# One fused conv-attention and mixture-of-experts kernel: order of ScalarE's token work, an earlier start of the token statistics, and a matrix product that adds the two output halves

## The reference, cut to what matters

```python
x = x + conv_attention(layernorm_c(x))        # 8 heads, 8x8 windows, plus a 3x3 local conv; q, k, v, out are 1x1
t = tokens(x)                                 # 8192 tokens of 64 numbers
gate_logits = layernorm(t) @ Wg + bg          # 8 experts
top_w, top_i = top_k(gate_logits, 2); top_w = softmax(top_w)
t = t + sum over the two experts e of top_w[e] * (gelu(layernorm(t) @ W1[e] + b1[e]) @ W2[e] + b2[e])
```

## Time and profile before

| | |
|---|---|
| median of 3 runs | 451.93 us (451.66 to 452.38) |
| the profiled execution, its own time | 450.36 us |
| its span, first to last instruction | 448.6 us |
| mean granted TensorE clock | 0.974 |
| busy PE, DVE, ACT, POOL | 409.8, 351.9, 334.9, 304.3 us |

### The profile page before, as it was taken

How to read it: one execution, slowest core, us unless ns; L and a number is a source line. 1 busy time by engine, 2 the same in 40 slices (tenths; PEclk the granted TensorE clock), 3 DMA queues, 4 the chain that set the end, 5 groups by cost and what they waited for, 6 DMA issues and landing times. The chain is left out here.

```text
span 448.6 us, 12510 instructions
## 1 busy us (share of the span) xinstructions
PE 409.8 (91%) x3921; PEld 277.0 (62%) x3921; DVE 351.9 (78%) x1240; ACT 334.9 (75%) x889; POOL 304.3 (68%) x406
## 2 busy tenths in 40 slices
PE   6897989899999899899899789698999999999995
PEld 5354434445454444445445345245999999999995
DVE  4688979977888978868969989888876688778532
ACT  2466688788877787777787665444988898888884
POOL 4233434775855889888888858466777777777765
PEclk8899989999999999989999899989999999999998
DMA  9916800000000000000000000014332222222310
GB/s 221 233 48 124 183 2 2 1 1 1 2 1 2 14 20 20 21 18 14 20 21 14 24 26 32 19 49 105 99 75 76 64 58 59 62 71 73 78 45 0
DMA packets 36168, 22.42 MB, mean 50 GB/s; under 512 B 13648, under 2 KB 33855, under 8 KB 36104
## 3 DMA queue, kind: packets, MB, share of 16 engines
q1 hardware_dynamic: 30264, 14.70, 14.7%
q0 software_dynamic: 4960, 6.45, 4.4%
q10 hardware_dynamic: 880, 0.48, 0.7%
HBM read 13.07 MB, written 9.27 MB: 50 GB/s over the span
## 5 line engine op out<-in xcount | busy, mean ns | idle before, releaser
L672 POOL TENSOR_TENSOR pn<-pe_,rs 128x512 f32<-128x512 f32 x64 | 67.2, 1050 | 65.4 <-DVE rs L1213 61.3
L1509 PE MATMUL bank<-aa,bd 64*64 64x256 f32 x512 | 70.5, 392 | 12.2 <-ACT pt L821 8.7
L642 POOL DMA_INDIRECT rows_hbm<-rowb,posu x64 | 65.7, 1026 | 23.2 <-issue 17.2
L687 POOL DMA_INDIRECT out<-bt,zs x63 | 62.8, 996 | 21.5 <-issue 16.1
L1512 PE MATMUL bank<-pt,bt 64*64 64x256 f32 x512 | 70.5, 393 | 0.0
L1202 DVE TENSOR_REDUCE mx<-bank 128x8 f32<-128x512 f32 x64 | 43.8, 684 | 31.4 <-PE bank L1509 31.0
L833 ACT ACTIVATE pe_<-sc 128x512 f32<-128x512 f32 x64 | 40.6, 635 | 33.2 <-DVE sc L1205 23.0
L1509 PEld LDWEIGHTS bank<-aa,bd 64*64 64x64 f32 x512 | 33.5, 133 | 46.0 <-issue 35.7
L793 ACT COPY zs<-bank 128x512 f32<-128x512 f32 x64 | 37.2, 581 | 15.0 <-PE bank L1512 14.9
L1205 DVE TENSOR_TENSOR sc<-bank,mx 128x512 f32<-128x512 f32 x64 | 44.2, 691 | 2.2
L1325 DVE SCALAR_TENSOR_TENSOR bt<-bank,zs 128x64 f32<-128x64 f32 x91 | 25.4, 280 | 25.6 <-PE bank L1692 24.3
(11 more groups left out here) (298 smaller groups left out, 1042.0 us busy)
## 6 DMA issues: line engine op xcount, KB each, us to landing
zs<-rows_hbm SPq DMA_DIRECT2D x91, 66.0 KB, 2.2
wloc<-in_L_conv_w_local SPq DMA_DIRECT2D x2, 1152.0 KB, 8.8
rows_hbm<-zrow SPq DMA_DIRECT2D x1, 1914.0 KB, 13.6
x_sb<-in_x SPq DMA_DIRECT2D x3, 512.0 KB, 10.9
wloc<-in_L_ffn_W SPq DMA_DIRECT2D x2, 512.0 KB, 6.8
rows_hbm<-rowb,posu POOLq DMA_INDIRECT x64
out<-bt,zs POOLq DMA_INDIRECT x63, 2.3
wrec<-in_w2b SPq DMA_DIRECT2D x1, 520.0 KB, 4.3
```

Of the source, the lines that this page charges most:

```text
L642: nc.gpsimd.indirect_dma_start(out=rows_hbm, out_offset=bass.IndirectOffsetOnAxis(ap=posu[:, t:t + 1], axis=0), in_=rowb[:, t], in_offset= ...
L672: nc.gpsimd.tensor_tensor(pn[:, v % 2, :].rearrange("p (h j) -> p h j", h=HEADS), pe_[:, v % 2], rs[:, v % 2].unsqueeze(2).broadcast_to([P ...
L687: nc.gpsimd.indirect_dma_start(out=out, out_offset=bass.IndirectOffsetOnAxis(ap=idx_j, axis=0), in_=ob[:, j % LANES], in_offset=None, boun ...
L1509: scored = nc.tensor.matmul(dots[v % 2][same, w * 2 * P:(w + 1) * 2 * P], xq[same, t % 2, 2 * v + w], aa[same, t % 2, :, j0:j0 + WT], star ...
```

## The change

Five edits. (1) `norm` of batches 0 to 4 is due at 0, 1, 2 slots behind the statistics, not at 1, 2, 3. (2) ACT does `token_halves` of batches 0 to 2 ahead of the exponential of the slot, not last in it. (3) ACT does `second_xs` of batches 0 to 4 behind the copy of `pt`, not ahead of it and of `xsp`. (4) PE multiplies `ys` by `halves32` (128 x 64, two stacked 64 x 64 identities), which transposes and adds the halves in one product with 64 columns, and DVE adds the residual in one instruction in place of two. (5) POOL builds `halves32` in two copies at the start, and `bt` shrinks to the 64 columns that are used.

```diff
-STEADY = dict(norm=(1, 2, 3), halves=(4, 5, 6, 7), low=(6, 8), ...
+STEADY = dict(norm=(0, 1, 2), halves=(4, 5, 6, 7), low=(6, 8), ...
...
-            pool.wait_ge(ident_ready, 7)
+            for k in range(2):
+                rows_k = slice(k * C, (k + 1) * C)
+                pool.wait_ge(ident_ready, 7 + k)
+                nc.gpsimd.tensor_copy(halves32[rows_k], ident[rows_k, rows_k]).then_inc(ident_ready, 1)
+            pool.wait_ge(ident_ready, 9)
...
                     values_out(g, u)
-                    for b, k in due("xs", g, u):
-                        if b <= 4:
-                            second_xs(b)
...
                         nc.scalar.copy(pt[:, v % 2], ptb[:].rearrange("p (a b) -> p a b", a=PAIRS)).then_inc(pt_ready, 1)
+                    for b, k in due("xs", g, u):
+                        if b <= 4:
+                            second_xs(b)
...
                         keys_out(nxt, 1)
+                    for b, k in due("halves", g, u):
+                        if b < 3:
+                            token_halves(b, k)
                     t, v = tile(g, u)
...
                     for b, k in due("halves", g, u):
-                        token_halves(b, k)
+                        if b > 2:
+                            token_halves(b, k)
...
-                        nc.vector.tensor_tensor(tmp[:, b], src[:, :, 0], xs, ALU.add).then_inc(x1_ready, 1)
-                        wait(dve, x1_ready, at(prv2, 2, 1))
-                        nc.vector.tensor_tensor(xd, src[:, :, 1], tmp[:, b], ALU.add).then_inc(x1_ready, 1)
+                        nc.vector.tensor_tensor(x1[:, bass.ds(idx(prv2, TG), TG), :], turn[YT][:, 0:TG * C].rearrange("p (t c) -> p t c", t=TG),
+                                                x_sb[:, bass.ds(idx(prv2, TG), TG), :], ALU.add).then_inc(x1_ready, 2)
...
                             for k in range(TG):
-                                last = nc.tensor.transpose(turn[YT][:, k * P:(k + 1) * P], ys[:, prv2 % 2, k * P:(k + 1) * P], ident[:])
+                                last = nc.tensor.matmul(turn[YT][:, k * C:(k + 1) * C], ys[:, prv2 % 2, k * P:(k + 1) * P], halves32[:],
+                                                        start=True, stop=True)
```

More of the change, by code:

```diff
@@ L107, in stats_slot @@
     return 4 * (BATCH[b][0] + BATCH[b][1] + 1) + 2
-STEADY = dict(norm=(1, 2, 3), halves=(4, 5, 6, 7), low=(6, 8), turned=9, xs=10, gate=11, gate_out=11, logits=11, top=(12, 12),
+STEADY = dict(norm=(0, 1, 2), halves=(4, 5, 6, 7), low=(6, 8), turned=9, xs=10, gate=11, gate_out=11, logits=11, top=(12, 12),
               index=(13, 13), classes=(13, 14), gaps=14, tanh=16, ranks=15, ranks_out=15, weights=17, place=17, counts=18,
@@ L180, in program @@
         both16 = sb("both16", [P, 2, C], F16)
+        halves32 = sb("halves32", [P, C])
         cst_sb = sb("cst_sb", [P, 6, CLS])
@@ L217, in program @@
         bd = sb("bd", [P, 2, TG * 2, 2, WT])
-        bt = sb("bt", [P, 2, TG * 2, P])
+        bt = sb("bt", [P, 2, TG * 2, C])
         aa = sb("aa", [P, 2, PAIRS, GT])
@@ L276, in program @@
         xq = bd[:, :, :, 0]
-        xw = bt[:, :, :, 0:C]
+        xw = bt[:]
         xr = zf[:, 0:SLOTS * ROW].rearrange("p (s r) -> p s r", s=SLOTS)
@@ L1222, in body @@
                     if u == 2 and real(prv2):
-                        src = turn[YT][:].rearrange("p (t k c) -> p t k c", t=TG, k=2)
-                        b = prv2 % 2
                         wait(dve, yt_done, at(prv2, 1, 1))
-                        xs = x_sb[:, bass.ds(idx(prv2, TG), TG), :]
-                        xd = x1[:, bass.ds(idx(prv2, TG), TG), :]
-                        nc.vector.tensor_tensor(tmp[:, b], src[:, :, 0], xs, ALU.add).then_inc(x1_ready, 1)
-                        wait(dve, x1_ready, at(prv2, 2, 1))
-                        nc.vector.tensor_tensor(xd, src[:, :, 1], tmp[:, b], ALU.add).then_inc(x1_ready, 1)
+                        nc.vector.tensor_tensor(x1[:, bass.ds(idx(prv2, TG), TG), :], turn[YT][:, 0:TG * C].rearrange("p (t c) -> p t c", t=TG),
+                                                x_sb[:, bass.ds(idx(prv2, TG), TG), :], ALU.add).then_inc(x1_ready, 2)
                         wait(dve, x1_ready, at(prv2, 2, 2))
@@ L1616, in body @@
                             wait(pe, y_ready, at(prv2, 1, 1))
+                            if is_step(prv2, 0):
+                                pe.wait_ge(ident_ready, 9)
                             for k in range(TG):
-                                last = nc.tensor.transpose(turn[YT][:, k * P:(k + 1) * P], ys[:, prv2 % 2, k * P:(k + 1) * P], ident[:])
+                                last = nc.tensor.matmul(turn[YT][:, k * C:(k + 1) * C], ys[:, prv2 % 2, k * P:(k + 1) * P], halves32[:],
+                                                        start=True, stop=True)
                             last.then_inc(yt_done, 1)
```

## The result

| | before | changed |
|---|---|---|
| median of 20 runs each | 451.31 us (448.63 to 454.02) | 458.05 us (451.31 to 465.7) |
| ratio to before, 95% interval | | 1.0076 [1.0045, 1.0107] |
| profiled execution, its own time | 450.36 us | 451.31 us |
| its span | 448.6 us | 449.5 us |
| its mean granted TensorE clock | 0.974 | 0.989 |

The forecast was 450.6 us. The changed kernel's times spread over 14 us, those of before over 5. The ratios here compare only runs within 1.5% of the fastest of their kernel, which leaves out 10 of the changed kernel's 20 and none of before, so that 1.0076, or 3.4 us, is less than the ratio of the medians. The profiled execution of the changed kernel is its fastest one. It had a better clock than the profiled one of before and was still 0.95 us slower.

The account below looks back on a forecast made before the run. The attention loop was taken as bound by what PE issues and, four times, a chain from POOL ending in `pt`. Terms summed to -0.2, the clock -1.15, so 451.93 - 1.35 = 450.6 us, range 448.0 to 454.0.

Parts of the forecast that it names:

- The product: PE's eight records in place of four transposes: 0.47 us more a group in 16 groups, +3.29 us where no wait hides it.
- The statistics one slot sooner: POOL's `pn` of tile 32 comes 1.45 to 1.6 us sooner; waits ahead of slots 36, 44, 52 shrink.
- the check of batches 3 and 4: POOL, slots 38, 39, 46: no or little idle time, `pn` of tiles 38, 39, 46, 47 up to 2.4 us later.
- The halves ahead of the exponential: ACT: -0.3 us from idle time in slot 28; exponential 0.8 to 1.2 us later in nine other slots, taken as nothing.
- D: Time of an event after the change less its time before, positive meaning later.
- `do_a` of slots 42 and 50: PE: new waits ahead of it there would show the forecast wrong; no size given.
- `second_xs`: ACT, placed behind the copy of `pt`: 0, since PE waited for `pt` in none of those slots.
- DVE's addition: One of two instructions goes, 0.4 us: -0.4 at the end and -0.4 in slots 14 to 17, nothing elsewhere.
- The clock: The dip at 188 to 194 us, behind slot 44's wait, goes: 1.6 us, less 0.45 taken back by POOL's chain, -1.15.
- The slower one: Rival: POOL's order in slots 38, 39, 46, 47 keeps waits ahead of 36, 44, 52; +2.2 us, 454.1 us, chance 0.23.
- The "faster" rival: All three waits ahead of slots 36, 44, 52 go and POOL costs nothing: -3.45 with the clock, 448.5 us, chance 0.15.
- -0.2: Whole loop and tail: the sum of the forecast's terms in us with the clock as it was.

Follow-up runs that it names:

- b3: Changed kernel with u=1 token halves last, behind `xw`, and POOL's token statistics behind the input's norm, product kept: 450.55 us, ratio 0.9972 to before.
- b4: Changed kernel with both orders mended (u=1 halves behind `xw`, statistics behind the input's norm), but the earlier four transposes and two DVE additions: 447.28 us, ratio 0.9921.
- a1: Kernel before with only PE's product by `halves32` and DVE's single addition: 452.34 us, ratio 1.0056.
- c1: Kernel before with PE's four transposes of `ys` replaced by plain f32 products with the 128x128 identity: one run, 460.8 us.
- a2: Kernel before with only the statistics one slot sooner: 450.56 us, ratio 1.0002.
- c3: b4 with `second_xs` back ahead of the copy of `pt`: 447.79 us, ratio 0.9936 to before.
- a3: Kernel before with only the token halves of batches 0 to 2 ahead of the exponential: 452.27 us, ratio 1.0033.
- b1: Changed kernel, but token halves in slots with u=1 stay last, behind `xw`: 454.03 us, ratio 1.0041 to before.
- a4_whole: The changed kernel again, unaltered, against the kernel before: 455.90 us, ratio 1.0097; its profiled execution took 460.07 us.

## Why the prediction was wrong, by its own steps

**The product** held. 128 records in eights; 0.40 us a group where 0.47 was taken. Slot 10 was to pay twice for its low stretch, which the profiled execution doesn't have. The sum of what is paid, 3.29 less 0.8 of DVE, is 2.5; b3 against b4 measured 3.3 in a kernel whose waits are gone, and a1 1.6 in the one where they take some of it. By the isolated gap of the Trainium skill (TensorE: Matmul & The Clock Gate, Back-to-back issue gap) the columns would have set it; c1 decides for the rows: 0.83 and 0.89 us with 64 and 128 columns, the width hardly matters.

**The statistics one slot sooner** gave more where it was meant to and lost it elsewhere. `pn` of tile 32 came at 151.86, with PE 2.11 us later than before; that is 151.23 + 2.11 - 151.86 = 1.5 us sooner, forecast 1.45 to 1.6. The waits ahead of slots 36, 44 and 52 went to 0.3, not to 0.1, 0.7 and 1.2. **A step that failed** is the check of batches 3 and 4: "only tiles 40 and 41 (48 and 49) come out even or ahead. POOL's queue (sends, their DMAs) is behind these parts and shifts with them". Only `pn` and the sends were followed. `hl`, which is in the same queue, and PE's transposes of it in slots 41 and 49 were not. In a2 this alone takes back 3.8 of 4.5 us.

**The halves ahead of the exponential** is the other failed step: "the exponential comes 0.8 to 1.2 us later. Its sum is due on DVE a slot later ... so I take nothing." The exponential itself was hidden as said: no wait for it appears. But `xw` is queued behind it, and PE wants that at once. It costs 0.47 + 1.05 + 1.05 us of waits, less 0.29 each in slots 30 and 38 for the waits for `aa` that it covers. The gain was right in size: D falls by 0.33 in slot 29, where 0.3 was taken. The prediction did name `do_a` of slots 42 and 50 as a place where it could fail, but for another chain; in the changed kernel the waits there are in 22, 30 and 38.

**`second_xs`, DVE's addition, the two copies at the start**: nothing seen against what was taken. c3 can't tell the first from zero. The single addition takes 0.42 us.

**The clock** was right at its place, by luck as far as the runs show, and wrong as a sum. The stretch behind slot 44 is gone in both traces of the changed kernel. But a1 kept a wait of 1.38 us ahead of slot 44 and a3 one of 1.74, and neither has a stretch behind it:

```profile
188.00:194.00 6.00, 5.32 (x51) 2.76 (x52) 4.71 (x28) 4.72 (x11) 5.61 (x7) 1.00 0.04 13
...
190.00:196.00 6.00, 5.15 (x50) 2.59 (x51) 4.43 (x27) 4.72 (x12) 5.61 (x7) 1.00 0.06 18
```

(a1_product, then a3_halves.) In slot 10 the same wait of 2.15 us has a low stretch behind it in one execution of the changed kernel and none in the other. Low stretches stand behind five of the eight waits for `hl` of 1.66 us and more in four traces: two of the changed kernel, a2's and b1's. So such a wait can be followed by one and need not be, and the 1.6 us taken off for the wait of slot 44 rested on one execution. What makes the changed kernel's runs spread over 14 us stays open beyond this: its two traces differ almost only by low stretches, but why it has so many long runs, and b4 none, isn't shown. The Trainium skill (the same page, Part 4: PE-mode transpose) would have fewer low stretches after transposes are replaced; a1 lost 9.2 us of clock on the mean of 12 runs and the kernel before 10.2, too little apart to say.

**The rivals.** The slower one, +2.2 us, had its place right, POOL in slots 38, 39, 46 and 47, and its path wrong: it went by `pn` and the exponential and said that the waits ahead of slots 36, 44 and 52 would stay. They went. The "faster" rival had that right. It assumed that POOL costs nothing. Where that was made true with the product kept, in b3, the kernel came out level with before, not 0.8% faster; that took leaving the product out, in b4.

**In sum**, at an equal clock, 3.8 to 4.5 us slower where -0.2 was forecast; the ratio gives 3.4. New waits not counted: slot 22 0.47, slots 30 and 38 2 x (1.05 - 0.29), slots 41 and 49 1.40 + 2.03, together 5.4 us. Against them, the waits ahead of slots 36, 44 and 52 kept 0.87 us where 0.1 + 0.7 + 1.2 = 2.0 were forecast, 1.1 less. -0.2 + 5.4 - 1.1 = +4.1, inside the first two. The rest, up to the 6.7 us between the medians of all runs, comes from the changed kernel's long runs, as far as its two traces show by low stretches; the forecast took 1.15 us off for the clock.

## What to carry to other kernels

When an instruction is moved ahead of another, list everything behind it in that queue up to its old place, short copies for other engines too, and follow each to the engine that waits for it; here two such copies, `xw` and `hl`, decided the sign. The time a step needs is not a price by itself, its place in a full queue is: the same edit made 3.8 us of waits for `hl` ahead of it and none behind it. And where the clock varies from run to run, neither one execution nor the wait ahead of one low stretch says what a change does to the clock: here one pair of profiles gave 0.95 us, the medians of 20 runs each 6.7.

## What the runs showed of the hardware that was not expected

- Plain f32 products with 128x128 weights are paid by the record, or by its weight load, and hardly by the column: eight records took 0.83 us with 64 columns and 0.89 with 128, four f32 transposes with 128 columns 0.43.
- The two traces of the changed kernel agree in each slot's length to 0.04 us wherever the clock is the same; 8.6 of the 8.8 us between them come at six places. A single profile can thus be compared slot by slot, if the low stretches are marked first.
- What a low stretch costs depends on where it falls: at the start of a4_whole's trace 6.9 us of lost clock moved the loop by 1.7 us, in slot 42 1.7 us lost moved it by 1.6.
- The same wait of PE can be followed by a low stretch in one execution and not in the next: 2.15 us in slot 10, with a stretch behind it in a4_whole and none in the other trace of the same kernel.
